# A graph attention, a linear attention and an expert layer on one core: edge items beside the mix's first pair

## What is computed

```
# branch 1: three graph attention layers, 4 heads of 192, 21250 edges, all from the same x1
x1 = relu(xn @ W_ah + b_ah)
h = (x1 @ W).reshape(N, 4, 192)
e = leaky_relu(as_n[src] + ad_n[dst], 0.2)      # per head
m = segment_max(e, dst); p = exp(e - m[dst]); s = segment_sum(p, dst)
out = segment_sum(p / (s[dst] + 1e-16) * h[src], dst) + b
y1 = relu(concat(relu(out_l) for l in 0..2) @ W_out + b_out)
# branch 2, "the mix": 12 heads of 64 with 256 random features
q, k, v = xn @ w_qkv.T
q', k' = ratio * (exp(norm * q @ proj.T - |q|^2 / 2 - max) + eps)    # max per row for q, over all for k
y2 = (q' @ (k'.T @ v) / (q' @ sum k')) @ w_proj.T + b_proj
x = x + y1 + y2
# then: softmax switch to one of 8 experts with a capacity, gelu MLP, added to x
```

## Time and profile before

| | us |
|---|---|
| median of 3 runs | 1648.24 (1646.88 to 1652.59) |
| the profiled execution | 1647.98 |
| its span | 1646.2 |
| TensorE busy | 1506.8 (92%) |
| VectorE busy | 1180.3 (72%) |
| ScalarE busy | 680.2 (41%) |
| gathers, line 1111 | 418.0, 2400 matmuls |
| edge maxima, line 1538 | 174.4, 120 |

### The profile page before, as it was taken

How to read it: one execution, slowest core, us unless ns; L and a number is a source line. 1 busy time by engine, 2 the same in 40 slices (tenths; PEclk the granted TensorE clock), 3 DMA queues, 4 the chain that set the end, 5 groups by cost and what they waited for, 6 DMA issues and landing times.

```text
span 1646.2 us, 26056 instructions
## 1 busy us (share of the span) xinstructions
PE 1506.8 (92%) x10187; PEld 1179.8 (72%) x10187; DVE 1180.3 (72%) x2646; ACT 680.2 (41%) x1369; POOL 434.3 (26%) x251
## 2 busy tenths in 40 slices
PE   2979999999989889899999989998999999985897
PEld 2556666555555678888988988888888986664786
DVE  6677673365668799998986797768766843787665
ACT  3430010122332667777777764335533531442110
POOL 3688888888810000000000000000000000001553
PEclk9999999999999989999999999999999999997999
DMA  9435544445475532434320354335322322762992
GB/s 352 100 69 108 111 93 86 88 77 110 107 243 133 154 79 72 124 100 124 91 68 29 106 165 165 112 112 191 123 74 74 101 61 74 259 235 78 343 296 75
DMA packets 194090, 212.42 MB, mean 129 GB/s; under 512 B 81521, under 2 KB 147259, under 8 KB 193968
## 3 DMA queue, kind: packets, MB, share of 16 engines
q1 hardware_dynamic: 117344, 185.71, 35.7%
q0 software_dynamic: 75760, 22.70, 8.6%
q10 hardware_dynamic: 864, 2.36, 0.4%
HBM read 144.09 MB, written 67.75 MB: 129 GB/s over the span
## 4 chain that ended last, share of the span: by engine, by line
PE 49%; POOL 17%; DVE 14%; DMA 9%; issue 6%; ACT 4%; SPq 1%; POOLq 0%; ACTq 0%; DVEq 0%
PE bank L1111 19%; POOL table L2189 17%; PE bank L937 6%; PE bank L939 6%; PE bank L938 6%; DMA table<-amount,place 4%; DVE junk L1538 3%; PE bank L1279 3%; PE bank L1147 2%; PE bank L1175 2%; PE bank L1128 2%; DVE eb L1573 2%; DVE eb L1582 1%; DMA tab<-table 1%; PE bank L1190 1%
## 5 line engine op out<-in xcount | busy, mean ns | idle before, releaser
L1111 PE MATMUL bank<-hb,eb 128*128 128x193 f32 (+3 forms) x2400 | 418.0, 331 | 13.9 <-ACT node L1992 9.3
L1111 PEld LDWEIGHTS bank<-hb,eb 128*128 128x128 f32 (+3 forms) x2400 | 398.7, 191 | 20.0 <-issue 10.6
L2189 POOL DMA_INDIRECT table<-amount,place x170 | 350.5, 2062 | 75.5 <-issue 48.1
L2195 POOL IOTA iota8i<- 128x8 int32 x1 | 0.1, 135 | 900.1 <-DMA node_rows<-node 900.1
L1573 DVE SCALAR_TENSOR_TENSOR eb<-shift_b,as_low,shift_b 128x640 f32<-128x640 f32 (+1 forms) x240 | 196.4, 860 | 0.3 <-PE bank L1111 0.2
L1978 ACT ACTIVATE eb<-eb,asd 128x640 f32<-128x640 f32 (+1 forms) x240 | 181.5, 813 | 28.7 <-DVE eb L1573 28.7
L1582 DVE SCALAR_TENSOR_TENSOR eb<-eb,count 128x1280 f32<-128x1280 f32 (+1 forms) x120 | 174.5, 1454 | 6.9 <-ACT eb L1978 6.9
L1538 DVE CUSTOM_DVE_ANT_0 junk<-ab,absent 128x1250 bf16<-128x1250 f32 x120 | 174.4, 1454 | 1.9
L937 PE MATMUL bank<-wg_hi,x1T_hi 128*128 128x384 bf16 (+3 forms) x360 | 118.9, 330 | 0.6 <-DVE x1T_lo L1394 0.6
L939 PE MATMUL bank<-wg_hi,x1T_lo 128*128 128x384 bf16 (+3 forms) x360 | 118.7, 330 | 0.0
L938 PE MATMUL bank<-wg_lo,x1T_hi 128*128 128x384 bf16 (+3 forms) x360 | 118.7, 330 | 0.0
(11 more groups left out here) (288 smaller groups left out, 3027.4 us busy)
## 6 DMA issues: line engine op xcount, KB each, us to landing
w<-in_w SPq DMA_DIRECT2D x16, 1152.0 KB, 11.3
shift_b<-shift_rows SPq DMA_DIRECT2D x24, 625.0 KB, 5.8
h_rows<-h_row SPq DMA_DIRECT2D x27, 388.0 KB
hb<-h_rows SPq DMA_DIRECT2D x12, 873.0 KB
ar<-node_rows SPq DMA_DIRECT2D x27, 384.0 KB
table<-zero POOLq DMA_DIRECT2D x3, 3054.0 KB, 19.7
tab<-table SPq DMA_DIRECT2D x27, 312.5 KB, 4.2
qk_rows<-qk_row SPq DMA_DIRECT2D x12, 625.0 KB
```

The source lines that it names most:

```text
L1111: ins = T.matmul(bank[w // 2][0:M, c0:c0 + GC + 1], p[0:K, u, w * P:w * P + M], hv[0:K, t, 0:GC + 1], start=opens and u == 0 and w % 2 == ...
L2189: G.indirect_dma_start(tables[i], bass.IndirectOffsetOnAxis(place[:, c:c + 1], axis=0), amount16[:, c:c + 1], None, compute_op=ALU.add).th ...
```

## The change

The step that spread maxima alone beside the first pair is gone, so items and maxima start together right after `head_in:0`. `evict` is held in the order until `first_pair`. `k_first` moves into the fifth `eb` buffer, `q_first` and `v_first` behind the buffers (where `rinv` and `node` are later), `junk` and one `count16` to another region. The waits follow: `edge_z` no longer waits for all of pair 0, but for the values' last copy, and from item 4 on for the key `dash`es; `evict` waits for pair 0's queries and values; `head_in` of head 0 waits only for the stored rows of h.

```diff
@@ graph_steps
     yield "head_in", 0
-    yield from spread(edges, lambda: FIRST_EDGE_RATE, lambda: "first_pair" in done)
     yield from paced((attention_steps(done), lambda: ATTENTION_RATE["mixed" in done]), (edges, lambda: EDGE_RATE["q" in done]))
@@ attention_steps
+    def evict(i):
+        if i % SPLITS == SPLITS - 1:
+            while "first_pair" not in done:
+                yield None
+            yield "evict", i // SPLITS
+
-    yield from in_step([(5, of_half("finish")), (5, mark), (4, of_half("evict")), (0, edge_z),
+    yield from in_step([(5, of_half("finish")), (5, mark), (4, evict), (0, edge_z),
@@ program, tiles
-        k_first, q_first = put("k_first", [128, 2, N], BF16), put("q_first", [128, 2, N], BF16)
-        v_first = put("v_first", [P, NT, 2, HD + 1])
-        after_first = cursor[0]
-        count16 = [put("count16_0", [P, N], BF16)]
-        assert cursor[0] <= r_d
+        after_wv = cursor[0]
         cursor[0] = r_c
         eb = [put(f"eb{i}", [P, 2, HN]) for i in range(EDGE_BUFFERS)]
+        after_eb = cursor[0]
         rinv = put("rinv", [P, 2, HALF])
         node = [put(f"node{i}", [P, HALF, HW]) for i in range(2)]
-        cursor[0] = after_first
-        junk = put("junk", [P, N], BF16)
+        assert cursor[0] <= r_d
+        cursor[0] = after_eb - size([P, 2, HN], F32)
+        assert cursor[0] >= after_wv
+        k_first = put("k_first", [128, 2, N], BF16)
+        cursor[0] = after_eb
+        q_first = put("q_first", [128, 2, N], BF16)
+        v_first = put("v_first", [P, NT, 2, HD + 1])
@@ VectorE, edge_z
-                ve.wait_ge("dash_mm", 2 * NT)
-                ve.wait_ge("feat_used", NT)
+                ve.wait_ge("v_copy", 2 * NT)
+                if i >= EDGE_BUFFERS - 1:
+                    ve.wait_ge("dash_mm", NT)
@@ ScalarE, evict
                 se.wait_ge(f"node_out{half}", (32 if half else 16) * (H // 2))
+                se.wait_ge("dash_mm", 2 * NT)
+                se.wait_ge("feat_used", NT)
@@ SyncE, head_in
-                second_over()
+                if lh:
+                    second_over()
+                else:
+                    for i in range(3):
+                        sy.wait_ge(f"h_out{i}", 16 * (NT * LAYERS // 3))
```

More of the change, by code:

```diff
@@ L771, in program @@
         cursor[0] = r_f - size([P, N], U16)
-        count16.append(put("count16_1", [P, N], BF16))
+        count16_1 = put("count16_1", [P, N], BF16)
         cursor[0] = r_e
@@ L791, in program @@
         shift, shift_t = put("shift", [P, TURN]), put("shift_t", [P, TURN])
-        mz, ms = put("mz", [P, NT]), put("ms", [P, NT])
-        cursor[0] = r_f + 9024
-        r_g = cursor[0]
+        m_sum = put("m_sum", [P, 2, NT])
+        mz, ms = (m_sum[:, i, :] for i in range(2))
+        r_g = r_f + 9024
+        at_junk = cursor[0]
+        junk = put("junk", [P, N], BF16)
+        cursor[0] = at_junk
+        count16 = [put("count16_0", [P, N], BF16), count16_1]
+        assert cursor[0] <= r_g + 32
+        cursor[0] = r_g
         ab = [put(f"ab{i}", [P, N]) for i in range(2)]
```

## The result

The changed kernel takes 1655.38 us (median of 20 runs, 1646.47 to 1660.58), the kernel before 1648.78 (20 runs, 1646.88 to 1653.48): a ratio of 1.0037, 95% interval 1.0025 to 1.005. It is slower by 0.4%, where 1638.6 us was forecast.

A forecast was written before the change was run, and what follows sets the result against it. VectorE was taken to bound pairs 1 to 4, TensorE pair 5's keys and the row blocks. Terms -26.2 - 2.4 + 14.3 + 1.5 + 1.7 + 1.5 = -9.6 us gave 1638.6 us, range 1630 to 1650.

The forecast's parts named there:

- Pair 0's cost: First pair: `edge_z:0` waits for shift rows, first `q_max` comes later, pair 1 begins later: +14.3 us, bounds +7 and +22.
- the clock term: First gather and first query tile: TensorE waits without fillers behind, its clock falls: +1.5 us, bounds -1 and +31.
- Pair 5: Pair 5's keys: six more maxima on VectorE, six elevenths of 3.2 us: +1.7 us, bounds 0 and +3.2.
- the row blocks: Eight gathers leave the row blocks, -26.2 us; layer 1's first tile is no longer covered, +1.5 us.
- the small edits: Moved tiles, `junk`, `count16` and the new waits of `evict`, `edge_z` and `head_in:1`: put at nothing.
- The rival that the tail gives nothing back: Stretch after 985 us not paced by TensorE's work: 28.6 us of gains go, costs stay, 1667 us; chance 0.03.
- the signs of being wrong: Pair 1 outside 602 to 617, a later pair changing over 3 us, clock under 0.85, waits above 3 before gathers.
- One stall may go: TensorE's 4.7 us wait before `gather:80`, behind weight copies, may vanish; half taken: -2.4 us, bounds -5 and +5.
- late rows or new stalls eat the gain: Rival: shift rows land at 553, an eviction caught between weight copies, pair 5 at +3.2: near 1647 us; chance 0.18.
- pairs 1 to 4, put at nothing: Pairs 1 to 4 hold the same counts of items and maxima as before, so their length changes by 0 us.
- count as nothing: The 40 dropped `warm_mix` matmuls of 512 columns lie in TensorE's slack beside pairs 0 and 1: no cost.

The follow-up runs named there:

- e1: Kernel before with the change's tile places and waits but the old order (maxima alone beside the first pair kept): ratio 0.9993 to the kernel before.
- e3: Changed kernel with the first two output weight loads issued beside pair 5's first query tiles: ratio 0.9988 to the kernel before.
- e7: Kernel before with the first two output weight loads issued beside pair 5's first query tiles: ratio 0.9992 to the kernel before.
- e9: Kernel before with each head's loads ordered beside item 7 instead of item 4 of the head before: ratio 1.002 to the kernel before.
- e5: Changed kernel with seven more maxima ordered at once behind `head_in:0`: ratio 1.0032 to the kernel before.
- e13: e5 with 0.6 maxima a tick beside pair 0: ratio 0.9986 to the kernel before.
- e8: Kernel before with the `warm_mix` fillers stopped after ten tiles of the mix: ratio 1.0052 to the kernel before.
- e10: Changed kernel with each head's loads ordered beside item 7 instead of item 4 of the head before: ratio 1.004 to the kernel before.

## Why the prediction was wrong

*Right, with size:* `edge_z:0` at 548.35 us after 12.14 us of idle (forecast 550 and 12):

```profile
548.35 0.89 DVE L1587 SCALAR_TENSOR_TENSOR eb<-shift_b,as_low,shift_b 128x640 f32<-128x640 f32 x1 [12.14 <-DMA shift_b<-shift_rows]
```

The first `q_max` came 30.6 us after the first `dash` (forecast 30.9) and pair 1 began at 610.5 (609.3). Pair 0's cost was 17.3 against 15.8 with the clock: from the first `q_max` it took 39.1 us, where pair 1's query half had given 35.75 and the clock term 1.5. TensorE's wait there was the one foreseen, and the clock fell to a mean of 0.65 between its two levels over 570 to 575 us and recovered:

```profile
573.19 1.12 PE L1173 MATMUL bank<-ident,ef 128*128 128x128 f32 x4 [4.35 <-ACT ef L2033]
...
570.00:575.00 5.00, 1.81 (x9) 1.57 (x10) 4.93 (x9) 1.64 (x5) 0.00 (x0) 0.65 0.69 215
```

Pair 5 (+1.8 against +1.7), the row blocks (-23.8 against -24.7) and the small edits at nothing (e1) held. The rival that the tail gives nothing back fell. Of the signs of being wrong, three did not come (pair 1 began inside 602 to 617, no later pair changed by over 3 us, the granted clock of 573 to 609 was 0.93), and the fourth did: a new wait above 3 us, the 6.1, before a gather.

*The step that failed* is "One stall may go ... I take half, **-2.4**, bounds -5 and +5". Its stretches came to +8.6 (7.7 and 0.9). The stall of 4.7 us before `gather:80` did go. But beside the second weight set TensorE now waits three times for `weigh`s, 6.1 us together, the longest behind a copy that waits 3.1 us for its transfer, so nothing is won there; and the new stall before `gather:55` stands ahead of it. The step looked at where each eviction falls among the weight copies, and said of `evict:10` that it "moves in between copies". It did not ask which *transfers* move: with items 8 further, `head_in:6` also comes right before the first output weights, on the same queue. The forecast followed the loads of `head_in:0` and `head_in:1`, and not those of the ten other heads. e3, e7 and e9 show the cause from both sides. The rival "late rows or new stalls eat the gain" names the mechanism but allowed +5 for it. With the term taken out by hand the forecast would have been -9.6 + 2.4 = -7.2 us; e3 measured -2 (-5.8 to +1.6).

*The terms that were a little too small* make about that difference: pair 0 by 1.5, pairs 1 to 4, put at nothing, by 2.4, pair 5 by 0.1, the row blocks by 0.9, together 4.9 us. The forecast of -9.6 and the +4.1 of the span differ by 13.7: the failed step 11.0, these 4.9, less 0.4 at the end and the 1.8 of the earlier start. How firm they are is another matter. Pairs 1 to 4 took 275.0 us in e5 and 274.2 in e13, with the same items and maxima in them as after's 277.9, and the old order had 273.7 to 277.1: their 2.4 us may be chance. And pair 0's term is measured against a trace of the kernel before in which the clock fell twice. e9 does the same work there, with the same wait before the same transposes, at a granted clock of 1.00 throughout, and takes 47.9 us:

```profile
586.15 0.56 PE L1160 MATMUL bank<-ident,ef 98*128 98x98 f32 x4 [1.81 <-ACT ef L2017]
```

So the wait of 1.8 us did not by itself bring the clock down, as the forecast's clock term took it, and against such an execution pair 0 costs 21.8 us, 6.0 more than forecast.

*Slips in the working, without weight:* pair 4's keys have nine more maxima than pair 5's had, so six of them are six ninths of 3.2, 2.1 us and not 1.7. The bounds of pair 0's term do not follow from what they name either: 570.5 and 30.7 us make +6.2 alone and some +13 with half of the items' work, not +7, and +14.3 with 3 and 3.2 us is 20.5, not 22. The measured values lie inside.

*A step that was wrong without harm:* fillers "count as nothing". In the old order they are worth some 8 us by the runs of e8 (4.8 to 12.4). In the changed one, with gathers in their place, the clock stood at 0.92 beside pair 0's queries and 0.97 in pair 1, and putting fillers back shortened neither, so the term held there without the reason given for it.

*What was not seen as a choice:* that the pace of the maxima was free. Moving items beside pair 0 without thinning the maxima there crowds VectorE; four fewer of them gave 10 us against e5 (e13), because pair 5 takes them at no cost.

## What to carry to other kernels

When a stream of work is shifted against another, list every transfer of both streams by its place in the queue before and after, and look for a large one that now stands right before a small one that somebody waits for; here a load issued early was the cure, and a shift by a few steps was not. Balance an engine's deferrable work over the stages by where that engine is the bound and let it end before the stretch in which others wait for it: here that was worth 0.5% in the old order and, with the change, early loads and fillers, 0.9%.

## What the hardware showed

Two matmuls of 512 columns a tick that nobody reads kept the granted clock at 0.90 and 0.89 beside pair 0's end and pair 1; without them it stood at 0.75 and 0.66, between the levels of 1.2 and 2.4 GHz (e8). The loss, 4.0 us, came in pair 1, where TensorE was busy for 32.8 of 35 us; pair 0, at a lower clock beside its queries, took 52.5 us against 52.4. The Trainium skill, "TensorE: Matmul & The Clock Gate", section "What's actually happening", has the throttled state as the default that activity lifts; the trace agrees. The clock is not the same in each execution, though: the old order's pair 0, with fillers, took 52.4 us with a granted clock of 0.68 in its last 10.4 us, and 47.9 in e7 and e9 with 1.00.

2.2 MB of loads delayed what was issued behind them by the landing: a weight tile's copy started 9.2 us behind the issue instead of at most 6.0 (e9). The issuing engine can lose time too: SyncE took 4.04 us to issue one transfer behind such loads (after; 0.61 in the kernel before) and 4.12 us for the last of the loads themselves (e10; 1.27 in after), with everything in its queue waiting. In e9 the issues behind the loads took 1.2 us at most, so the loads alone do not make an issue long, and what does is open.
